# Two expert layers on one core: the experts' down products as three reduced-precision passes, a shorter ring of slot rows, one buffer of normalized rows

## The reference

```python
x = x + 0.5 * ffn(layernorm(x)); x = x + attention(layernorm(x)); x = x + 0.5 * ffn(layernorm(x))
# ffn, 16 experts, HIDDEN 256, INTER 128:
probs = softmax(x @ gate_w.T); topk_w, topk_idx = top_k(probs, 4); topk_w /= sum(topk_w)
scores = scatter of topk_w to 16 columns
g = einsum('th,ehi->tei', x, w1); u = einsum('th,ehi->tei', x, w3)
expert_out = einsum('tei,eih->teh', silu(g) * u, w2)      # the down product
out = einsum('teh,te->th', expert_out, scores)
```

## Time and profile before

| | |
|---|---|
| median of 3 runs (lowest to highest) | 1554.47 us (1553.87 to 1563.98) |
| profiled execution: its time / span of instructions | 1555.55 us / 1553.3 us |
| TensorE matmul rows busy | 1406.9 us, 91% of the span |
| TensorE weight loads busy | 959.1 us, 62% |
| VectorE / ScalarE / GpSimd busy | 1034.1 us, 67% / 776.2 us, 50% / 640.3 us, 41% |
| pairs of the first / of the third layer, first to last transpose | 152.8 to 384.8 us / 1252.2 to 1487.7 us |

### The profile page before, as it was taken

One profiled execution on the slowest core, in us unless ns is written; L12 is line 12 of the kernel. 1 busy time (PEld: TensorE's weight loads), 2 busy tenths in 40 slices (PEclk: granted clock), 3 DMA queues, 4 the chain that ended last, 5 costly groups with the idle time before them and its releaser, 6 DMA issues. The chain is left out here.

```text
span 1553.3 us, 30220 instructions
## 1 busy us (share of the span) xinstructions
PE 1406.9 (91%) x9796; PEld 959.1 (62%) x9796; DVE 1034.1 (67%) x2636; ACT 776.2 (50%) x1317; POOL 640.3 (41%) x679
## 2 busy tenths in 40 slices
PE   4899999999978769999999999999689999999997
PEld 3777888889856623333333333333367878888886
DVE  5665646366788768888788788786267574544567
ACT  4412566555135524666566566567451245655530
POOL 3371443767644460222222222223245316076665
PEclk9899999999989967999999999999789999999999
DMA  7651566878326920353334343300131227588773
GB/s 255 229 204 55 178 196 191 261 244 256 109 58 176 232 82 1 58 68 43 42 43 66 44 57 43 42 2 2 57 104 64 82 93 237 155 265 244 245 230 108
DMA packets 159210, 198.94 MB, mean 128 GB/s; under 512 B 18180, under 2 KB 132440, under 8 KB 159064
## 3 DMA queue, kind: packets, MB, share of 16 engines
q1 hardware_dynamic: 140632, 146.67, 36.0%
q0 software_dynamic: 18432, 50.36, 10.3%
HBM read 105.21 MB, written 91.49 MB: 127 GB/s over the span
## 5 line engine op out<-in xcount | busy, mean ns | idle before, releaser
L1625 ACT ACTIVATE attn_prob<-attn_b_ps 128x1024 f32<-128x1024 f32 (+3 forms) x352 | 304.0, 870 | 206.0 <-PE attn_b_ps L1826 204.9
L505 POOL DMA_INDIRECT xs_dram<-ffn_xn,ffn_index x192 | 189.1, 985 | 229.5 <-DVE ffn_index L780 173.2
L1806 PE MATMUL attn_a_ps<-k_rows,q_rows 96*128 96x512 bf16 (+3 forms) x768 | 249.7, 348 | 22.7 <-DVEq L1663 7.3
L519 POOL DMA_INDIRECT ffn_gathered<-ys_dram,ffn_index x192 | 196.0, 1021 | 89.6 <-issue 55.6
L1676 DVE TENSOR_REDUCE attn_max_a<-attn_a_ps 128x1 f32<-128x512 f32 (+2 forms) x304 | 202.8, 688 | 41.9 <-PE attn_a_ps L1806 26.4
L1565 POOL TENSOR_SCALAR_AFFINE_SELECT attn_prob<-attn_prob 128x512 f32<-128x512 f32 x128 | 81.3, 636 | 349.7 <-ACT attn_prob L1625 347.6
L824 DVE TENSOR_TENSOR ffn_xs_lo<-ffn_xt_ps,ffn_xs_hi 128x512 fp32r<-128x512 f32 x144 | 97.7, 678 | 156.7 <-ACT ffn_xs_hi L596 154.7
L1806 PEld LDWEIGHTS attn_a_ps<-k_rows,q_rows 96*128 96x128 bf16 x768 | 74.6, 98 | 187.3 <-DVE attn_max_a L1676 72.9
L1850 PE MATMUL attn_o_ps<-attn_prob,attn_v_now 128*17 128x256 f32 (+1 forms) x2560 | 188.0, 367 | 0.0
L1826 PE MATMUL attn_b_ps<-q_rows,k_rows 98*128 98x512 bf16 (+3 forms) x768 | 186.4, 331 | 0.3 <-ACT attn_prob L1625 0.3
L1673 DVE CUSTOM_DVE_ANT_0 attn_scored<-attn_a_ps,mask_wide 128x512 bf16<-128x512 f32 (+1 forms) x256 | 154.6, 623 | 33.2 <-PE attn_a_ps L1806 28.7
(11 more groups left out here) (209 smaller groups left out, 2723.5 us busy)
## 6 DMA issues: line engine op xcount, KB each, us to landing
ffn_xs<-xs_dram SPq DMA_DIRECT2D x138, 256.0 KB, 3.9
ys_dram<-ffn_y SPq DMA_DIRECT2D x138, 256.0 KB, 2.9
xs_dram<-ffn_y SPq DMA_DIRECT2D x16, 768.0 KB, 11.0
qk_parts<-proj_cut SPq DMA_DIRECT2D x32, 384.0 KB, 3.2
k_rows<-qk_parts SPq DMA_DIRECT2D x96, 128.0 KB, 4.8
q_rows<-qk_parts SPq DMA_DIRECT2D x96, 128.0 KB, 7.4
ffn_w_stage<-in_L_ffn_w_dram SPq DMA_DIRECT2D x64, 128.0 KB, 2.5
x_res<-in_L_attn_x_dram SPq DMA_DIRECT2D x4, 1024.0 KB, 8.1
```

The source lines that it names most:

```text
L505: pool.indirect_dma_start(xs_dram[(b + 1) % 2], bass.IndirectOffsetOnAxis(index[:, b, i, k:k + 1], 0), xn[:, b % 2, i, :], None, bounds_ch ...
L519: pool.indirect_dma_start(gathered[:, t % G_RING, k, :], None, ys_dram[b], bass.IndirectOffsetOnAxis(index[:, b, i, k:k + 1], 0), bounds_c ...
L1625: act.activation(prob[PROB[kt]][:, h:h + heads, prob_at(kt, kt * P):prob_at(kt, S)], b_ps[:, slot, :].rearrange("p (h t) -> p h t", h=head ...
L1806: ins = pe.matmul(a_ps[:, bank, i * keys:end], q_rows[q][0:SROWS, h0 + i, qt * P:(qt + 1) * P], k_rows[q][0:SROWS, h0 + i, first:first + k ...
```

## The change

Six edits, all in `ffn`:

1. `w_down` is held as `w_down_hi` and `w_down_lo` (float32r). ScalarE copies the high part and GpSimd subtracts the low one (`cut_down`, four times). The raw weights are loaded into entries of the ring `xs`, so SyncE starts loading pairs only after the last of these cuts, and the loads of parts 2 and 3 wait for the cuts of parts 0 and 1.
2. The gated values are cut as well: in the pairs by ScalarE (`act_hi`, in place of the copy `act_t`) and VectorE (`act_lo`, new); in the dense steps by a new copy on ScalarE and a new subtraction on VectorE (`dense_cut`), written over `xs_hi` and `xs_lo`.
3. Each down product is `three_passes` instead of one float32 matmul.
4. `XS_RING` is 4, it was 5.
5. `xn` has one buffer, it had two: normalizing block b waits for the turns of block b - 1 and, from block 2 on, for the end of its scatter. Gated values are written over `silu`; `base`, `passed`, `same` and `gate_rows` share memory with others.
6. The product that counts the chosen experts (`count_before`) stands one offset later, and with it everything behind it; the fronts of blocks 2 and 3 and the combines begin 1 to 3 steps later. The last combines of block 2 fall into the tail. In a pair step ScalarE now cuts the activations before it does its part of a front.

```diff
@@ -45,13 +45,13 @@
...
 GU = 2 * INTER
-XS_RING, Y_RING, G_RING = 5, 3, 4
-OFFSETS = 16
+XS_RING, Y_RING, G_RING = 4, 3, 4
+OFFSETS = 17
 HEAD, TAIL = 21, 11
-ROOT_AT = {1: 7, 2: 6}
+ROOT_AT = {1: 7}
 MOMENTS_AT = 45
-FIRST, SECOND, THIRD = 2, 13, 14
-COMBINE = {1: (47, 50, 54, 57), 2: (61, 64, 68, 71), 3: (3, 6, 8, 11)}
+FIRST, SECOND, THIRD = 2, 14, 17
+COMBINE = {1: (50, 53, 57, 60), 2: (64, 67, 70, N + 1), 3: (N + 4, N + 7, N + 9, N + 12)}
 H, DH = 16, 16
@@ -240,15 +240,15 @@
...
-        w_down = sb("w_down", [P, E, D], F32)
-        gate_rows = sb("gate_rows", [E, D], F32)
+        w_down_hi = sb("w_down_hi", [P, E, D], F32R)
+        w_down_lo = sb("w_down_lo", [P, E, D], F32R)
...
-        xn = sb("xn", [P, 2, BT, D], F32)
+        xn = sb("xn", [P, BT, D], F32)
@@ -395,7 +405,9 @@
...
                 es = slice(i * E // 4, (i + 1) * E // 4)
-                sp.dma_start(w_down[:, es, :], w2[es].rearrange("e p d -> p e d")).then_inc(w_down_loaded[i], 16)
+                if i >= 2:
+                    sp.wait_ge(w_down_lo_ready, i - 1)
+                sp.dma_start(down_stage(i), w2[es].rearrange("e p d -> p e d")).then_inc(w_down_loaded[i], 16)
@@ -449,6 +461,7 @@
...
+            sp.wait_ge(w_down_lo_ready, 4)
             for n in range(XS_RING):
@@ -491,6 +504,12 @@
...
+
+            def cut_down(i):
+                pool.wait_ge(w_down_hi_ready, i + 1)
+                es = slice(i * E // 4, (i + 1) * E // 4)
+                pool.tensor_tensor(w_down_lo[:, es, :], down_stage(i), w_down_hi[:, es, :].bitcast(F32),
+                                   ALU.subtract).then_inc(w_down_lo_ready, 1)
@@ -547,15 +570,20 @@
...
+            def cut_down(i):
+                act.wait_ge(w_down_loaded[i], 16)
+                es = slice(i * E // 4, (i + 1) * E // 4)
+                act.activation(w_down_hi[:, es, :], down_stage(i), ACT.Copy).then_inc(w_down_hi_ready, 1)
+
             def normalize(b, i):
...
                         act.wait_ge(rstd_ready, b + 1 - made)
+                    if b >= 1:
+                        act.wait_ge(turned, b * BT)
                     if b >= 2:
-                        act.wait_ge(turned, (b - 1) * BT)
-                    if b == 3:
-                        act.wait_ge(scattered[1], 16 * BT * TOP_K * (nth + 1))
-                act.activation(xn[:, b % 2, i, :], x_res[:, b * BT + i, :], ACT.Identity, bias=nmr[:, b % 2, i:i + 1],
+                        act.wait_ge(scattered[b - 1], 16 * BT * TOP_K * (nth + 1))
+                act.activation(xn[:, i, :], x_res[:, b * BT + i, :], ACT.Identity, bias=nmr[:, b % 2, i:i + 1],
                                scale=rstd[:, b % 2, i:i + 1]).then_inc(xn_ready, 1)
@@ -592,23 +620,27 @@
...
                     act.wait_ge(gu_ready, n - 1)
+                else:
+                    act.wait_ge(o_ready, 2 * HEAD)
                 w = tiles_of(n) * D
...
                 if n >= 2:
-                    act.wait_ge(act_ready, n - 1)
+                    act.wait_ge(act_turned, n - 1)
+                else:
+                    act.wait_ge(dense_lo_ready, HEAD)
                 t = tiles_of(n)
...
-            def copy_act(n):
+            def cut_act(n):
                 act.wait_ge(act_turned, n + 1)
...
                 w = tiles_of(n) * P
-                act.activation(act_t[:, n % 2, 0:w], at_ps[:, 0:w], ACT.Copy).then_inc(act_t_ready, 1)
+                act.activation(act_hi[:, n % 2, 0:w], at_ps[:, 0:w], ACT.Copy).then_inc(act_hi_ready, 1)
@@ -623,8 +655,18 @@
...
-                    act.wait_ge(dense_act_ready, k - 1)
+                    act.wait_ge(dense_lo_ready, k - 1)
+                if k == HEAD:
+                    act.wait_ge(act_turned, N)
...
+
+            def dense_cut(k):
+                act.wait_ge(dense_act_ready, k + 1)
+                if k >= 2:
+                    act.wait_ge(o_ready, 2 * (k - 1))
+                if k == HEAD:
+                    act.wait_ge(gu_ready, N)
+                act.activation(xs_hi[:, k % 2, :], silu[:, k % 2, :], ACT.Copy).then_inc(dense_hi_ready, 1)
@@ -656,15 +702,16 @@
...
                 if 0 <= n + 1 < N:
                     gate(n + 1)
+                if 0 <= n < N:
+                    cut_act(n)
                 for b, o in slot_offsets(n):
                     front_make(b, o)
                     front_take(b, o, 1)
-                if 0 <= n < N:
-                    copy_act(n)
                 if 0 <= n - 1 < N:
                     copy_y(n - 1)
             for e in range(TAIL):
                 dense_gate(HEAD + e)
+                dense_cut(HEAD + e)
         @block.vector
@@ -798,7 +845,7 @@
...
             parts = {0: early_stats, 1: late_stats, 3: inverse_root, 8: router, 9: compare, 10: choose, 11: weigh,
-                     12: count, 13: place_rows, 14: place_experts, 15: place_scores}
+                     13: count, 14: place_rows, 15: place_experts, 16: place_scores}
@@ -840,8 +887,19 @@
...
                     dve.wait_ge(act_turned, N)
-                dve.tensor_tensor(act_f[:, k % 2, :], gu_ps[:, k % 2, :, :].rearrange("p j c -> p (j c)"), silu[:, k % 2, :],
+                dve.tensor_tensor(silu[:, k % 2, :], gu_ps[:, k % 2, :, :].rearrange("p j c -> p (j c)"), silu[:, k % 2, :],
                                   ALU.mult).then_inc(dense_act_ready, 1)
+
+            def cut_act(n):
+                dve.wait_ge(act_hi_ready, n + 1)
+                w = tiles_of(n) * P
+                dve.tensor_tensor(act_lo[:, n % 2, 0:w], at_ps[:, 0:w], act_hi[:, n % 2, 0:w].bitcast(F32),
+                                  ALU.subtract).then_inc(act_lo_ready, 1)
+
+            def dense_cut(k):
+                dve.wait_ge(dense_hi_ready, k + 1)
+                dve.tensor_tensor(xs_lo[:, k % 2, :], silu[:, k % 2, :], xs_hi[:, k % 2, :].bitcast(F32),
+                                  ALU.subtract).then_inc(dense_lo_ready, 1)
@@ -904,10 +965,14 @@
...
                     add_dense(HEAD + e - 1, 0)
+                if e < TAIL:
+                    dense_cut(HEAD + e)
+                if 0 < e <= TAIL:
                     add_dense(HEAD + e - 1, 1)
-                for late in range(2):
-                    if e - late in COMBINE[3]:
-                        combine(3, 2 * COMBINE[3].index(e - late), late)
+                for b in (2, 3):
+                    for late in range(2):
+                        if N + 1 + e - late in COMBINE[b]:
+                            combine(b, 2 * COMBINE[b].index(N + 1 + e - late), late)
@@ -942,7 +1007,7 @@
...
                     turn(b, i)
-                if o == 11 and late:
+                if o == 12 and late:
                     count_before(b)
@@ -969,16 +1034,17 @@
...
                 e = k % E
                 if j == 0:
-                    pe.wait_ge(dense_act_ready, k + 1)
+                    pe.wait_ge(dense_lo_ready, k + 1)
                     if k < E and e % 4 == 0:
-                        pe.wait_ge(w_down_loaded[e // 4], 16)
+                        pe.wait_ge(w_down_lo_ready, e // 4 + 1)
                 if k >= 1:
                     pe.wait_ge(o_added, 2 * (k - 1) + j + 1)
...
                 for i in range(half_tiles):
                     at = (j * half_tiles + i) * P
-                    ins = pe.matmul(y_ps[:, j, i, :], act_f[:, k % 2, at:at + P], w_down[:, e, :], start=True, stop=True)
+                    ins = three_passes(pe, y_ps[:, j, i, :], xs_hi[:, k % 2, at:at + P], xs_lo[:, k % 2, at:at + P],
+                                       w_down_hi[:, e, :], w_down_lo[:, e, :], True, True)
                 ins.then_inc(o_ready, 1)
@@ -1015,26 +1081,27 @@
...
                 if n >= 1:
-                    pe.wait_ge(act_t_ready, n)
+                    pe.wait_ge(act_lo_ready, n)
                 for j in range(tiles_of(n)):
-                    ins = pe.transpose(at_ps[:, j * P:(j + 1) * P], act_f[:, n % 2, j * INTER:(j + 1) * INTER], ident[:, :])
+                    ins = pe.transpose(at_ps[:, j * P:(j + 1) * P], silu[:, n % 2, j * INTER:(j + 1) * INTER], ident[:, :])
                 ins.then_inc(act_turned, 1)
...
             def down(n, of):
-                pe.wait_ge(act_t_ready, n + 1)
+                pe.wait_ge(act_lo_ready, n + 1)
                 if n >= 2:
...
                 for j in range(tiles_of(n)):
-                    ins = pe.matmul(y_ps[:, n % 2, j, :], act_t[:, n % 2, j * P:(j + 1) * P],
-                                    w_down[:, bass.ds(of[j], 1), :].rearrange("p a d -> p (a d)"), start=True, stop=True)
+                    hi, lo = (t[:, bass.ds(of[j], 1), :].rearrange("p a d -> p (a d)") for t in (w_down_hi, w_down_lo))
+                    ins = three_passes(pe, y_ps[:, n % 2, j, :], act_hi[:, n % 2, j * P:(j + 1) * P],
+                                       act_lo[:, n % 2, j * P:(j + 1) * P], hi, lo, True, True)
                 ins.then_inc(y_ready, 1)
...
                 for h in range(KT):
```

(19 more changed lines are left out.)

21 lines of the change are left out of this document (14 added, 7 removed).

## The result

| | before | after |
|---|---|---|
| median of 4 runs (lowest to highest), us | 1554.17 (1553.09 to 1563.98) | 1750.32 (1747.75 to 1763.93) |
| span of the profiled execution, us | 1553.3 | 1746.0 |
| mean granted clock | 0.961 | 0.937 |

The change makes the kernel slower: ratio 1.1252, 95% interval 1.1216 to 1.1287, +196 us. 1685 was forecast, and the range ended at 1735.

The account below looks back on a forecast made before the run. TensorE was taken to set the pace nearly everywhere. Profiled execution 1555.55 us, + 132 for the ring of four with the pairs' saving already taken out, + 0 for dense steps, gave 1687.6, stated as 1685; range 1605 to 1735.

Parts of the forecast that it names:

- What bounds, and ring of four: Pair steps: TensorE sets the pace; with four entries practically every load is late, 4.27 us a step against 3.27, +132 us.
- The signs it named: Transposes waiting for `ffn_xs` 50 to 80 us, pair step about 4.3 us, stretches near 298 us, activations waiting behind register loads.
- the terms of its loop: Two pair steps: 0.95 to down product's end, 1.23 to load issue, 3.5 landing, 2.85 to activations; sum 8.53 us.
- Dense steps: Head and tail: three-pass products save 0.31 us a step where TensorE bounds, VectorE's subtraction costs 690 ns; sum 0 per layer.
- -5.6 + 2.6 - 1 + 2 + 2 = 0: Dense us per layer: shorter products, tail combine steps, head's front steps, one buffer of rows, new chain at the ends.
- I put these five at -1: Head's five steps with block 1's front: the count product's wait goes, VectorE's work fills the gap; -1 us per layer.
- One buffer of rows: Head: ScalarE normalizes block 2 only after block 1's scatter lands; between 0 and 4.5 us, taken as +2 per layer.
- no wait: Pairs: block 3 is normalized 15 pair steps, over 60 us, after block 2's index is known, so no wait counted.
- Count product: Head: its wait of up to 6.0 us for the choice of experts goes, as it stands one offset later.
- Down products in pairs: Pair steps: six passes of 0.71 us replace float32 products of 0.95, -0.24 us a step; unstalled steps 2.8 to about 3.3.
- No gain, no loss: Rival: pair loads in time, but the sequencer holds the step at 3.1 to 3.3 us; 1540 to 1570 us, chance 0.03.
- The clock: Rival: waiting in pair steps drops the granted clock to 1.2 GHz, steps about 5.6 us, 1882 us; chance 0.04.

Follow-up runs that it names:

- b_ring4: The kernel before with one edit, the ring xs of four buffers instead of five: 1695.87 us, ratio 1.0914.
- a_order: The changed kernel with SyncE issuing the store of pair n-3 behind the load of pair n+4, ring still four: 1661.08 us, ratio 1.0683.
- b_ring4_order: b_ring4 with SyncE's new order, the store of pair n-3 behind the load of pair n+4: 1548.09 us, ratio 0.9952.
- a_cutlate: The changed kernel with the head's cut of gated values behind the front steps, on ScalarE and VectorE: 1728.78 us, ratio 1.1109.
- b_xn1: b_noassert with one buffer of normalized rows, block 3's front and the combines 3 steps later, its root between the scatters: 1559.94 us, ratio 1.0034.
- b_rest: b_xn1 with the ring of four and SyncE's new order, down products still float32: 1559.32 us, ratio 1.0015.
- a_noassert: a_both without the range check of the register loads of expert numbers: 1588.59 us, ratio 1.0206.
- a_both: The changed kernel with both the edits of a_order and a_cutlate: 1632.65 us, ratio 1.0478.
- b_noassert: The kernel before without the range check of the register loads of expert numbers: 1539.85 us, ratio 0.991.
- b_order_noassert: b_noassert with SyncE's new order of loads and stores, ring of five: 1532.45 us, ratio 0.9862.
- a_all: a_noassert with ScalarE's cut of the down weights in the head's odd steps, ahead of the up weights' cut: 1588.21 us, ratio 1.0206.

## Why the prediction was wrong

**What bounds, and ring of four: right in mechanism, partly lucky in size.** +132 us was forecast for the ring; b_ring4 shows +143 in the pairs, the changed kernel +141. The signs it named are there: 68 waits for `ffn_xs` with 60.4 us (50 to 80), pair stretches of 303.9 and 304.7 us (298), the sequencer's register loads in the open behind a wait. The issue behind the store was the right place (a_order, b_ring4_order). But the terms of its loop are not as good as its sum. The median landing was 3.1 us where 3.5 was taken, and TensorE waited for slots in 68 of 142 steps, about half, where the text had "practically every load". The forecast 4.27 us a step and the measured 4.28 (303.9 / 71) agree in part by luck; which term made good for these two no run shows. The Trainium skill (DMA: Bandwidth & Descriptors, section Anatomy of one DMA) has 2.6 us for 256 KB, as a fit for transfers that GpSimd starts, while SyncE starts these. It is lower than any median of these loads (3.0 to 4.1 us over all runs); by it the step would have been an estimated 3.8 us.

**Dense steps: the sum "-5.6 + 2.6 - 1 + 2 + 2 = 0" is the step that failed.** It was +20 and +21 us per layer in the heads, +3 in the tails, 47 in all; without them the result would lie near 1703 us. The plain steps did go from 4.54 to 4.21 us, as forecast. What was missing is ScalarE's place in the five front steps: only VectorE's added work was counted there ("I put these five at -1"). The new cut on ScalarE cost 0.63 us of work, but it waits for VectorE, and behind it in order stood the rows that TensorE's logits were waiting for. a_cutlate puts it last and gets 24.6 of the 41 us back. Of the other 17, b_xn1 and b_rest put about 2 us per head with the single buffer, and a_noassert against b_rest 11 us of both heads with the three passes' cuts and the later count, not separated. The prediction had the failure in its list of signs (dense steps that grow by microseconds because ScalarE waits), but for a scatter, and without a price.

**One buffer of rows: "+2 per layer", "no wait" for block 3.** About right for the slow kernel: ScalarE waited at most 2.4 us for a scatter, and b_xn1's heads are 2 us longer each. It is wrong as soon as the pairs are fast: with the moved front and combines b_xn1 shows +20 us in all.

**Count product: the wait "goes".** It did not: there are two waits of up to 8.3 us where six of up to 6.0 had been, 16.3 us in all from 17.3. With the cut put last (a_cutlate) the longest is 5.9 again, so what was over 6.0 came from the cut.

**Down products in pairs: -0.24 us a step, with the sequencer as its limit.** The limit held, the saving was too high. From the first pass to the next pair's transposes it is 0.79 us in a_noassert, not 0.71, and the float32 products take 0.86 in b_rest, without the check, not 0.95. With the activations' transposes before them the gain is 0.15 us a step. With the check the sequencer takes it back and more: the step of a_order is 3.36 us, a little over the "2.8 to about 3.3" of the text. The check's price is 44 us with ring and cut mended. In the changed kernel itself the pairs grew by no more than b_ring4's, so the sequencer's cost and the late loads overlap there and don't add.

**The rivals.** "No gain, no loss" described in kind what the pairs do once the loads are in time, with 3.1 to 3.3 us for a step that is 3.36 in a_order, but the 47 us of loss there weren't in it. The clock didn't fall in the pairs: 0.98 and 0.97 granted, with a quarter of the time idle. In the heads it did, to 0.88.

So 196 us are: 141 in the pairs (the ring behind the stores; mending it alone leaves 47, and dropping the range check then takes 49 off), 41 in the heads (25 by the cut's place in ScalarE's order), 6 in the tails, the rest spread.

## What to carry to other kernels

A ring's depth is only as good as the place of its loads in the queue that issues them: before paying for another buffer, or giving one up, move the load ahead of the store that it stands behind. When an operation is added to an engine that works in order, list who waits for what stands *behind* it, not only what it costs. And splitting a product into passes multiplies instructions: where addresses come from registers, count the sequencer's work per step beside the matmuls', and drop range checks for values that are already clipped. Compare such a split with a kernel that has the same limits taken away, or it gets credit for them.

## What the runs showed of the hardware

- TensorE's sequencer is a bound of its own. Two register loads with their range checks fill 302.7 to 303.9, 1.2 us of a step of 3.36 us; the median of the 282 loads is 0.31 us in a_order and 0.30 in the kernel before. Taking out a 151 ns operation and an 18 ns check twice a step saved 44 us over 142 steps, 0.31 us a step, about their own length (0.34).
- A sequencer-bound step hardly shows in the busy view: TensorE is busy for 223 of 257 us in a_both's first pairs. The row to look for is "<- issue" before the first instruction behind a register load, 109 times in it. And that row understates: 6.5 us in the kernel before, where b_noassert gained 15.
- The time from issue to landing of the same 256 KB loads moves between kernels, and not with their speed alone: the page's median is 3.1 us in the changed kernel, 3.9 in the kernel before, 4.1 in b_order_noassert, the fastest kernel, but 3.0 in a_noassert and 3.9 in a_all, which are equally fast. A ring's slack can't be counted from one trace's median to better than a microsecond.
